# How far the row gathers of the attention layer may run ahead of its score stages

## The reference

```
h = (x @ W).reshape(n, 8, 32)
a_src = einsum('nhc,hc->nh', h, att_src);  a_dst = ... att_dst
e = leaky_relu(a_src[src] + a_dst[dst], 0.2)      # one score per edge and head
m = segment_max(e, dst);  e = exp(e - m[dst])
alpha = e / segment_sum(e, dst)[dst]
out = segment_sum(h[src] * alpha, dst)            # weighted sum of the rows of h
x = layernorm(x + LN(out + bias) * gamma + beta)
```

## Time and profile before

| what | value |
|---|---|
| the profiled execution | 2973.91 us, its span 2972.1 us |
| median of three | 2973.91 us |
| PE busy in the span | 2471.2 us (83%) |
| DVE busy | 1395.9 us (47%) |
| POOL busy | 942.3 us (32%) |
| gathers of this line (L2132) | 376 and 40, of which 232 are staged |
| part that the change touches | 2192.8 us (first gather) to 2545 us (last staged rows kept) |

### The profile page before, as it was taken

One profiled execution on the slowest core, in us unless ns is written; L12 is line 12 of the kernel. 1 busy time (PEld: TensorE's weight loads), 2 busy tenths in 40 slices (PEclk: granted clock), 3 DMA queues, 4 the chain that ended last, 5 costly groups with the idle time before them and its releaser, 6 DMA issues. The chain is left out here.

```text
span 2972.1 us, 32381 instructions
## 1 busy us (share of the span) xinstructions
PE 2471.2 (83%) x9483; PEld 1625.7 (55%) x9484; DVE 1395.9 (47%) x3940; ACT 709.8 (24%) x1552; POOL 942.3 (32%) x927
## 2 busy tenths in 40 slices
PE   3677789898887999999999999999978887457770
PEld 2444788343666555565556555577744434346560
DVE  7999655355575001030101001355566664546668
ACT  3777545111443000010001000155400000103112
POOL 0000256666666100000000000012257666766740
PEclk9888989999988999999999999999988998678995
DMA  6565678343333744434444434333648888646641
GB/s 234 245 253 225 217 229 262 105 142 112 110 107 108 177 154 134 153 126 154 133 153 134 142 123 146 101 104 99 124 147 266 276 292 251 225 130 194 191 127 43
DMA packets 209534, 493.89 MB, mean 166 GB/s; under 512 B 46457, under 2 KB 128430, under 8 KB 209134
## 3 DMA queue, kind: packets, MB, share of 16 engines
q1 hardware_dynamic: 135185, 301.30, 32.2%
q10 hardware_dynamic: 38173, 133.27, 12.8%
q0 software_dynamic: 36032, 57.60, 7.2%
HBM read 374.71 MB, written 117.32 MB: 166 GB/s over the span
## 5 line engine op out<-in xcount | busy, mean ns | idle before, releaser
L792 POOL DMA_INDIRECT table_dense_weights<-pair_weight,dst x416 | 412.1, 991 | 568.3 <-DVE weights_c L847 328.2
L1524 PE MATMUL banks<-own_term,features_and_rows 128*128 128x391 f32 (+1 forms) x1656 | 552.3, 491 | 0.0
L2132 POOL DMA_INDIRECT features_and_rows<-table_heads,src x376 | 406.3, 1081 | 177.2 <-issue 100.4
L1524 PEld LDWEIGHTS banks<-own_term,features_and_rows 128*128 128x128 f32 x1656 | 312.2, 189 | 226.8
L1550 DVE TENSOR_SCALAR features_and_rows<-banks,hop_bias 128x391 f32<-128x391 f32 (+1 forms) x24 | 15.0, 625 | 761.5 <-PE banks L1524 761.5
L952 PE MATMUL banks<-split_rows,count_columns 128*128 128x512 f32 x1200 | 322.5, 417 | 15.5 <-ACT count_columns L934 11.9
L2529 PE MATMUL banks<-features_and_rows,edge_to_window 128*128 x880 | 231.9, 425 | 105.1 <-DVE edge_to_window L2490 81.2
L1524 PE MATMUL banks<-features_and_rows 128*128 128x391 f32 (+1 forms) x840 | 282.4, 491 | 0.0
L952 PEld LDWEIGHTS banks<-split_rows,count_columns 128*128 128x128 f32 x1200 | 230.4, 196 | 68.7 <-ACT count_columns L934 11.9
L2529 PEld LDWEIGHTS banks<-features_and_rows,edge_to_window 128*128 128x128 f32 x880 | 179.8, 209 | 157.3 <-issue 123.8
L558 PE MATMUL banks<-features_and_rows,pair_and_bias_rows 128*128 128x400 f16 x806 | 182.3, 386 | 88.5 <-DVE features_and_rows L540 50.4
(11 more groups left out here) (425 smaller groups left out, 2948.7 us busy)
## 6 DMA issues: line engine op xcount, KB each, us to landing
hidden<-table_counts SPq DMA_DIRECT2D x305, 160.0 KB
table_dense_weights<-weights_c ACTq DMA_DIRECT2D x26, 1600.0 KB, 5.7
own_term<-table_dense_weights SPq DMA_DIRECT2D x52, 782.0 KB
features_and_rows<-table_rows_by_edge SPq DMA_DIRECT2D x58, 528.0 KB
own_term<-table_dense_weights SPq DMA_DIRECT2D x34, 780.5 KB
pair_and_bias_rows<-table_edge_rows ACTq DMA_DIRECT2D x50, 512.0 KB
weights_c<-table_edge_rows ACTq DMA_DIRECT2D x50, 512.0 KB
table_rows_by_edge<-features_and_rows SPq DMA_DIRECT2D x48, 528.0 KB
```

The source lines that it names most:

```text
L792: e.indirect_dma_start(out=self.table, out_offset=bass.IndirectOffsetOnAxis(ap=self.place[:, t:t + 1], axis=0), in_=self.values[:, t:t + 1 ...
L1524: m = e.matmul(psum[b][:, 0:wide], z_block(block)[:, f * P:(f + 1) * P], streamed[tile % STREAM][:, lo - from_column:lo - from_column + wi ...
L2132: e.indirect_dma_start(out=to[:, k, :], out_offset=None, in_=t_h, in_offset=bass.IndirectOffsetOnAxis(ap=src[:, t:t + 1], axis=0)).then_in ...
```

## The change

The number of stages by which a group may be ahead goes from 3 to 14. And of the four gathers of a group the first and the third alone wait for the stages, both on `s_masked`; the second and the fourth waited on `s_first` before, the semaphore of the six matmuls of the next stage.

```diff
-        STAGES_BEHIND = 3
+        STAGES_BEHIND = 14
         def gather_group(e, quad, to, sem, stage=0):
             for k in range(GROUP):
                 t = quad * GROUP + k
-                if stage + k // 2 > 0:
-                    e.wait_ge(s_first if k % 2 else s_masked, min(stage + k // 2 + k % 2, len(STAGES)))
+                if k % 2 == 0 and stage + k // 2 > 0:
+                    e.wait_ge(s_masked, stage + k // 2)
                 e.indirect_dma_start(out=to[:, k, :], ...).then_inc(sem, 16)
```

## The result

The changed kernel took 3010.43 us (median of 4 runs, 3007.92 to 3016.49), the one before 2973.66 us on the same chip (4 runs): ratio 1.012, 95% interval 1.009 to 1.015. It is slower by 1.2%, outside the range of the prediction. The profiled executions, 3005.63 us (span 3003.8) and 2973.91 us (span 2972.1), differ by 31.7 us.

The account below looks back on a forecast made before the run. No engine was full between 2291.2 and 2488 us; DMA was fullest, at a share of 0.86. Free-running stages +14 and the tail -8 made +6 us on 2973.91: 2980 us, range 2960 to 2998.

Parts of the forecast that it names:

- 0.31 us more for each of 45 stages, +14: Stages while POOL runs free after group 16: 3.20 us each instead of 2.89, over 45 stages, +14 us.
- The lead: POOL's lead over the stages from group 16: grows 0.4 stage a group, 11 stages in some 28 groups, 143 us.
- point 1: POOL's waits at L2132 from 2290 us: nearly vanish for some 28 groups and come back around 2430.
- point 2: Masks in the 197 us after 2291: about 63, not 68.
- The DMA check: DMA queues before mask 100: 18.4 us of moved work costs 0 if it fits the gaps, 21 us if none does.
- Rival B: Index loads at L2083: with POOL not held, every stall is met by more gathers; +21 us, 2995; chance 0.2.
- The rule on how DMA engines take turns: Index loads beside two full queues: packet-wise turns would land a load in about 5 us; the measured stall seemed against it.
- The tail: Last eleven stages: 12 gathers beside them in place of 22, so 22 us for 30.3, -8 us, ends -12 and -3.
- point 3: First gather of the last group: starts some 25 us ahead of the last mask, not 1.3 after it.
- point 4: The eleven last masks: take about 22 us.
- The odd gates: Removed waits on `s_first` for second and fourth gathers: below 1 us in the mean, taken as 0, with an end of +3.
- The end as a block: After the last mask: no stage gates it, so it moves unchanged, 93.5 us to quad 16's gather as before.

Follow-up runs that it names:

- half_rows: The changed kernel with staged gathers fetching half a row a descriptor from the seventh group on, same number of gathers; ratio 1.010 to the kernel before.
- near_even_gates: The kernel before, still 3 stages, with the odd gathers' waits on `s_first` removed; ratio 1.004 to the kernel before.
- far_spaced: The changed kernel with POOL waiting before each of groups 10 to 21 until the rows of the group before have landed; ratio 1.022 to the kernel before.
- ctl_after: Control: the changed kernel with a bitwise AND that changes nothing on five register values engines wait against; 3020.08 us, ratio 1.010 to the kernel before.
- near_free_window: The kernel before, 3 stages, but with groups 30 to 37 not gated (24 stages for them); ratio 1.011 to the kernel before.
- ctl_before: Control: the kernel before with a bitwise AND that changes nothing on five register values engines wait against; 2996.60 us, ratio 1.002 to the kernel before.
- far_spacer: The changed kernel with a one-column POOL memset before each staged gather but those of group 7; ratio 1.012 to the kernel before.

## Why the prediction was wrong

The forecast was 2980, with 2998 as the edge. By its own steps:

- **The step that failed is "0.31 us more for each of 45 stages, +14".** It took the pace of the stages while POOL was free (3.20 us) for a steady price and its largest stall for an index load late behind gathers. With POOL free the stages don't go at 3.20 us: within some 16 gathers of an even stream PE's completions are held, and in the longer streams a stage takes about 20 us. The term measured +29 us in eight stages, in both pairs (62.2 - 33.4; 62.6 - 33.5), and +40.7 and +32.3 from the first gather to mask 96, in place of 14. The rate of 3.20 was a mean over stages in which DVE's additions lengthened some of POOL's gathers (up to stage 24) and one stall, which ended while the old gate held POOL for 3.2 us. It was made of that stall: without the 11.9 us between the two masks of the earlier trace rows the other 17 stages of the 57.6 us took 2.69 us each, less than the 2.89 they were set against.
- **What ends it.** The lead was to grow by 0.4 stage a group over 28 groups. It grew to 14 in eight groups (14 to 22), because the stages nearly stood; POOL met the gate at 2331 and was held 6.87 us at 2338.55, not from 2430 (point 1 wrong). The gate's distance sets how long POOL may stream into a stall: 16 gathers in a row with 3 stages, 33 with 8, 39 with 14.
- **The masks** from 2291.2 to 2488 were 52, not 63 (point 2 wrong).
- **The DMA check** (18.4 us of work moved, 0 to 21 us) measured a resource that wasn't short: the share fell from 0.83 to 0.74. Its two ends were taken for the bounds of the step, and so the range was too narrow. Rival B named a slower result of 2995 by the right place on POOL, "every stall is met by more gathers", but by the wrong mechanism; the empty queue of the index loads and half_rows refute it.
- **The rule on how DMA engines take turns** between queues, told from the Trainium skill's DMA: Bandwidth & Descriptors (Queues, rings and completion order), wasn't contradicted by the stall after all: with no load in the queue, the stall has nothing to say on it, and no run here tests it.
- **The tail** was -8, with ends -12 and -3. The last eleven stages took 16.6 us instead of 30.3, -13.7, and from mask 96 on -9.7 and -12.4 in the two pairs. Right in sign and kind. The last group began 17.1 us ahead of the last mask, not 25 (point 3), and the eleven stages took less than the 22 of point 4.
- **The odd gates** at 0 to +3: near_even_gates lies 0.2%, about 6 us, above its control, with intervals that overlap; not settled.
- **The end as a block** (point 5): quad 16's gather came at 2668.13, 95.5 us after the last mask, against 93.5. Right. The 49.52 us of the chain that nothing explained have the look of the stall in the merge (16 matmuls in 35 us above), and shortening that gained nothing, so counting it as 0 was right.

What the profile of before held against the forecast: at the stall of the earlier trace rows PE's six matmuls of L2224 end by the records at 2285.09 us and `s_first` rises at 2290.32, and from 2284.6 to 2290.2 the index loads' queue had this (packets, MB, share):

```profile
q10 hardware_dynamic: 5, 0.02, 0.9%
```

Nothing was late in it. I had read the wait by the instruction that came after it, not by what its semaphore waited for; and the earlier trace rows showed the same symptom beside POOL's longest run of gathers.

Open is by what PE is held. The runs show the place (the end of PE's last matmul to its semaphore), the condition (POOL issuing indirect DMAs evenly 1.25 us apart for some 20 us; whether it is the missing rest, the pace or the number of descriptors isn't settled, for the 31 gathers 1.61 us apart in the mean had no rest either and no stall) and what it isn't (bytes, index loads, PE's clock on its own: it is at 1.2 GHz in these stretches, 0.54 of full in the mean, but far_spaced shows it at 1.00 beside a POOL that rests, and in ctl_after it fell at 2299.5 us, when the wait that ended at 2301.55 had lasted for 5 us).

## What to carry to other kernels

A gate that ties a DMA-issuing engine to a consumer's progress can be worth its waits, as here, because it rests that engine when the consumer stalls; before loosening one, ask what happens if both feed back on each other. Read a stall from both its ends: when the last instruction that raises the semaphore was issued, and what the queue of the suspected load moved in the stall, before a mean rate over it goes into a sum; and take the stall out of that mean, to see what is left of the rate. A resource whose share falls during a stall is a poor suspect for it.

## What the runs showed of the hardware

- The profiles of the twenty kernels have 36 mask gaps of over 9 us. By the end of 29 of them POOL has issued 15 to 93 indirect DMAs of a stream; at the other seven 1 to 13. With four gathers under way, where POOL rested up to 3.8 us at a time, there were none.
- The longer the stream of staged gathers, the longer the worst gap in it. In those of 15 or 16 the largest gap was 4.9 to 11.2 us, so not each has a stall; in those of 17 to 23 it was 10.5 to 14.7; in all nine of 30 or more it was 18.1 to 44.0.
- The times between long stalls' masks are near whole multiples of 0.70 us: the masks of far_spaced above follow at 44.80 and 22.40, those of near_free_window at 20.99, of ctl_after at 21.00, of after at 20.31 us (64, 32, 30, 30 and 29 times). All ten times of over 20 us lie within 0.03 us of one; among the shorter of the 36 three are off by 0.13 to 0.14. Nothing in the runs says what has this period.
- The completions come late without POOL moving much: 18 GB/s in the merge of ctl_before.
- Between two gathers POOL has 0.3 us in which a memset of one column (0.11 us) is free: the gathers of far_spacer stay 1.25 us apart.
